# A Mamba mixer and a mixture of experts on one core: routing moved into the mixer's half-steps, the shared expert beside the final sum

## The chip, the cores and the metric

The kernel is one program on one core of a Trainium2 chip. The metric is the device time in microseconds (us) of one execution. Engines are called as in the profile: PE (TensorE), DVE (VectorE), ACT (ScalarE), POOL (GpSimd), SP (SyncE, which issues most DMAs).

## The reference

Two batches of 4096 tokens, 256 features, go through one adaptive-layernorm block of a mixer and a mixture of experts:

```python
mod = (silu(c) @ wmod).reshape(2, 6, 1, 256)       # sa, ca, ga, sb, cb, gb; ga, gb kept at least 0.25 from zero
h = layernorm(x) * (1 + ca) + sa
y = mamba2(h) + h                                  # in-projection, conv of 4 taps, scan over 8 heads x 64 x 128 states,
                                                   # gate by silu(z), rms norm, out-projection
g = y @ glu_w + glu_b;  y = y + g[:256] * sigmoid(g[256:])
x = x + ga * (layernorm(y) * ln_w + ln_b)
h = layernorm(x) * (1 + cb) + sb
scores = sigmoid(h @ gate_w.T);  idx = top4(scores + gate_b);  w = 2.5 * scores[idx] / sum(scores[idx])
y = sum_e w_e * (silu(h @ w1_e) * (h @ w3_e)) @ w2_e      # 16 experts, 4 per token, inner width 128
y = y + (silu(h @ w1_s) * (h @ w3_s)) @ w2_s              # shared expert
out = x + gb * y
```

## The kernel before

Matmuls with weights are made of three products of a high and a low part (`split3`, L102), so a weight or an input is split before its use: ACT makes the high part, DVE or POOL the low part. The engines run by semaphores; each engine's order of work is written out by hand, and an instruction that waits holds all that stands behind it on its engine. `nc.Block` borders, and `clear_semaphores` (L82), are barriers of all engines. The stages in order:

**Setup** (`setup`, L115): DMAs of c, `wmod` and the layernorm weights; ACT takes silu, PE makes the modulation as columns (`mod`) and as rows (the gates), DVE brings them into form.

**Token pass** (`prepare_tokens`, L202): 16 groups of 512 tokens. DVE takes statistics and normalizes, PE turns the tokens (`turn`, L306), ACT modulates, the result goes to `h_dram`; the mixer's weights are split between the groups, and dt and the decays of all tokens are made at the end and stored.

**Mixer** (`mixer`, L464): each batch has 16 steps of 256 tokens (CH = 2 chunks of 128). Both batches run as a pipeline of half-steps: `half(first, second, tail)` (L598 and below) works on three positions at once, the in-projection and conv of one step, the scan of another, the output part of a third; two half-steps advance both batches by one. Each engine has its own `half` with its order: SP L644, PE L796, ACT L927, DVE L1103, POOL L1193. Steps in it that matter below: SP's `load_halves` fills `hN` one half-step ahead, `load_h` fills `hT` (same data) for the residual add; `split_h` splits `hN` into `hTh` and `hTl` (L838 on ACT, L1163 on POOL) for PE's `project_xbc`; `split_y1` makes `y1h` and `y1l` for `glu`; `shift_x` (L1187) prepares the residual; `gated` (L1065), `norm2` and `apply2` (L1087) end the tail; `from_state` (L740) reads the state; `decays` (L882) makes exponentials. The bank names are shared: each batch has four PSUM banks, `Q(b, 0)` to `Q(b, 3)`. The output of the tail, `xr`, goes to `x2_dram`.

**Route** (`route`, L1252): 16 groups of 512 tokens. Loads x2, normalizes and modulates it, takes the scores of 16 experts (`logits`), DVE chooses four (`choose`, `weigh`), PE counts places (`positions`), DVE makes destinations (`assign`), ACT copies each token's row four times with its id and weight beside it (`take_rows`), and POOL scatters them to `xs_dram` with 16 indirect DMAs of 128 rows per group (`scatter`, L1647), sorted by expert. The shared expert is computed for the group too, times the gate, added to x2 and stored to `x2s_dram`, and one expert's weights are loaded (`raw`) and split per group.

**Plan** (`plan`, L1668): from the counts of tokens per expert, a table of 136 pairs of blocks and their weight offsets, read into registers later. **Blocks** (`blocks`, L1761): 136 pairs of 128-row blocks: turn, up, gate, down, scale by the weight, and two indirect scatters of rows to `ys_dram`. **Combine** (`combine`, L2013): 64 tiles of 128 tokens: adds the four expert rows, times the gate, plus `x2s_dram`, to `out`.

Of the kernel before, what the change touches and what calls it, by code (L numbers as in the profile page):

```python
# [16 lines left out]
ALU = mybir.AluOpType  # L17
# [5 lines left out]
NB = 2  # L23
# [25 lines left out]
SERIES = [1.0 / (2 * n + 1) for n in range(8, -1, -1)]  # L49


def build(nc, t, x2_dram, h_dram, par_dram, x2s_dram, xs_dram, ys_dram, out):
# [36 lines left out]
    with ctx:  # L89
# [6 lines left out]
        setup(nc, sem, t, mod, gate_b_row, gate_ln, ident, minus_half, bank)  # L96
        mixer(nc, sem, prime, t, mod, gate_ln, ident, minus_half, bank, h_dram, par_dram, x2_dram)
        clear_semaphores()
        experts(nc, sem, t, mod, gate_b_row, ident, minus_half, bank, x2_dram, x2s_dram, xs_dram, ys_dram, out)
# [15 lines left out]
def setup(nc, sem, t, mod, gate_b_row, gate_ln, ident, minus_half, bank):  # L115

    with ExitStack() as ctx:
        c_col = ctx.enter_context(nc.sbuf_tensor("c_col", [P, KD, NB], F32))
        c_silu = ctx.enter_context(nc.sbuf_tensor("c_silu", [P, KD, NB], F32))
        c_wide = ctx.enter_context(nc.sbuf_tensor("c_wide", [P, KD, NB, P], F32))  # L120
        wmod = ctx.enter_context(nc.sbuf_tensor("wmod", [P, KD, 6 * D], F32))
        pos = ctx.enter_context(nc.sbuf_tensor("pos", [P, 2, D], F32))
        mag = ctx.enter_context(nc.sbuf_tensor("mag", [P, 2, D], F32))
        lnw = ctx.enter_context(nc.sbuf_tensor("lnw", [P, 2, D], F32))
        loaded = sem("mod_loaded")
        silu_done = sem("c_silu_done")
        wide_done = sem("c_wide_done")
        cols_done = sem("mod_cols_done")
        rows_done = sem("mod_rows_done")
        link = sem("mod_link")  # L130
        with nc.Block() as block:
            @block.sync
            def _(sp):
                sp.dma_start(c_col[:, :, :], t["c_col"]).then_inc(loaded, 16)
                sp.dma_start(wmod[:, :, :], t["wmod"]).then_inc(loaded, 16)
                sp.dma_start(ident[:, :], t["ident"]).then_inc(loaded, 16)
                sp.dma_start(lnw[:, :, :], t["ln_wb"]).then_inc(loaded, 16)

            @block.gpsimd
            def _(pool):  # L140
                pool.memset(minus_half[:, :], -0.5)
# [2016 lines left out]
```

## Time and profile before

| | |
|---|---|
| median of 3 timed runs | 2222.96 us (2219.68 to 2231.39) |
| profiled execution, its own time | 2228.17 us |
| its span in the profile | 2226.4 us |
| mean granted TensorE clock | 0.859 |
| busy: PE, DVE, ACT, POOL | 74%, 66%, 47%, 45% |
| moved by DMA | 242.12 MB |

A busy share is that of the span; the clock is 1.0 for 2.4 GHz and 0.5 for 1.2 GHz. The rows that matter stand below, in their section, cut by stage.

### The profile page before, as it was taken

How to read it: one execution, taken by the hardware profiler on the slowest of the kernel's cores; microseconds unless marked ns; L12 is line 12 of the kernel's file. 1: busy time of each engine (PE TensorE's matmuls, PEld its weight loads, DVE VectorE, ACT ScalarE, POOL GpSimd, SP SyncE). 2: the span in 40 equal slices, each digit the busy share in tenths (PEclk: the TensorE clock that was granted, in tenths of full speed). 3: DMA queues.
4: the chain of work that ended last, by engine and by line, in shares of the span. 5: the costliest groups of instructions: out<-in, count | busy, mean ns of one | idle time of the engine just before them, and what ended most of it. 6: DMA issues, size and time to landing. Idle time of an engine off the chain costs nothing. (4 is left out here: it accounts for less than half of the span.)

```text
span 2226.4 us, 37571 instructions
## 1 busy us (share of the span) xinstructions
PE 1658.3 (74%) x10724; PEld 1424.5 (64%) x10725; DVE 1479.1 (66%) x3407; ACT 1053.1 (47%) x2135; POOL 1005.1 (45%) x905
## 2 busy tenths in 40 slices
PE   4757989988999889989887456565319999999300
PEld 4745777777777777777776455454319999999300
DVE  4635788878887788788876566666424444444488
ACT  1315556555655665565564334343206666665200
POOL 1202434443444444334443377777735666666300
PEclk7558999999999999999999666666659999999755
DMA  5421101110111011011010345454334555555599
GB/s 175 153 80 45 35 25 39 39 34 25 39 34 38 26 39 34 24 39 34 29 30 15 115 147 173 145 168 153 131 122 149 177 174 172 176 173 167 211 402 361
DMA packets 148926, 242.12 MB, mean 109 GB/s; under 512 B 24960, under 2 KB 95616, under 8 KB 148608
## 3 DMA queue, kind: packets, MB, share of 16 engines
q1 hardware_dynamic: 122752, 169.77, 24.1%
q0 software_dynamic: 26112, 71.62, 8.8%
q8 instruction: 27, 0.44, 0.1%
q14 instruction: 35, 0.29, 0.0%
HBM read 132.75 MB, written 108.56 MB: 108 GB/s over the span
## 5 line engine op out<-in xcount | busy, mean ns | idle before, releaser
L1997 POOL DMA_INDIRECT ys_dram<-byo,bx x272 | 261.3, 961 | 171.6 <-ACT byo L1930 94.6
L985 DVE SCALAR_TENSOR_TENSOR cv<-xc,convw,cv 128x256 f32<-128x256 f32 x576 | 294.3, 575 | 20.8 <-ACT cv L856 20.8
L1652 POOL DMA_INDIRECT xs_dram<-rows,dest x256 | 264.2, 1032 | 91.9 <-issue 77.1
L1173 POOL TENSOR_TENSOR state<-state,par 128x512 f32<-128x512 f32 x64 | 126.0, 1968 | 283.0 <-PE bank L746 283.0
L1966 DVE TENSOR_TENSOR bff<-bgs,bank 128x256 f32<-128x256 f32 x136 | 57.3, 421 | 212.8 <-ACT bgs L1914 212.8
L1930 ACT ACTIVATE byo<-bank,bx 128x256 f32<-128x256 f32 x272 | 114.3, 472 | 145.3 <-DMA ys_dram<-byo,bx 145.0
L104 PE MATMUL bank<-wh,bhh 128*128 x544 | 160.7, 295 | 8.1 <-ACT bhh L1907 6.0
L106 PE MATMUL bank<-wh,bhl 128*128 x544 | 154.3, 284 | 0.0
L105 PE MATMUL bank<-wl,bhh 128*128 x544 | 153.8, 283 | 0.0
L1184 POOL TENSOR_TENSOR y1l<-y,y1h 128x512 fp32r<-128x512 f32 x32 | 76.2, 2382 | 155.3 <-ACT y1h L912 155.3
L721 PE MATMUL bank<-masked,after 128*128 128x512 f32 x256 | 124.6, 610 | 21.4 <-ACT dec L886 21.4
L104 PE MATMUL bank<-hTh,win_hi 128*128 128x256 f32 x384 | 126.8, 330 | 15.8 <-POOL hTl L1166 15.8
L894 ACT ACTIVATE xdt<-yy 128x512 f32<-128x512 f32 x64 | 40.2, 628 | 192.9 <-POOL yy L1179 192.9
L735 PE MATMUL bank<-xdt,dec 128*128 128x64 f32 x1024 | 121.4, 272 | 0.0
L1179 POOL TENSOR_TENSOR yy<-yy,zs 128x512 f32<-128x512 f32 x64 | 87.6, 1369 | 73.6 <-DVE yy L1039 73.6
L1363 PE MATMUL bank<-ident,xn 128*128 128x128 f32 x128 | 31.5, 427 | 119.3 <-DVE xn L1519 119.3
L735 PEld LDWEIGHTS bank<-xdt,dec 128*128 128x128 f32 x1024 | 119.5, 192 | 0.0
L1907 ACT ACTIVATE bhh<-bank 128x512 fp32r<-128x512 f32 x136 | 83.3, 612 | 74.1 <-PE bank L1838 74.1
L104 PEld LDWEIGHTS bank<-wh,bhh 128*128 128x128 f32 x544 | 103.1, 190 | 18.1 <-issue 17.0
L1957 DVE TENSOR_TENSOR bhl<-bank,bhh 128x512 fp32r<-128x512 f32 x136 | 94.1, 692 | 28.0 <-ACT bhh L1907 24.4
L105 PE MATMUL bank<-hTl,win_hi 128*128 128x256 f32 x384 | 109.5, 285 | 0.0
L106 PE MATMUL bank<-hTh,win_lo 128*128 128x256 f32 x384 | 109.2, 284 | 0.0
(257 smaller groups left out, 5514.0 us busy)
## 6 DMA issues: line engine op xcount, KB each, us to landing
bx<-xs_dram SPq DMA_DIRECT2D x272, 129.0 KB
cy<-ys_dram SPq DMA_DIRECT2D x64, 512.0 KB, 9.2
px<-in_x SPq DMA_DIRECT2D x16, 512.0 KB, 3.6
h_t<-phT SPq DMA_DIRECT2D x16, 512.0 KB, 4.1
hN<-h_t SPq DMA_DIRECT2D x32, 256.0 KB, 2.7
hT<-h_t SPq DMA_DIRECT2D x32, 256.0 KB, 2.6
xr<-in_x SPq DMA_DIRECT2D x32, 256.0 KB, 2.6
x_dram<-xr SPq DMA_DIRECT2D x32, 256.0 KB, 2.0
```

Of the source, the lines that this page charges most:

```text
L104: pe.matmul(out, a_hi, b_hi, start=start, stop=False, skip_group_check=True)
L105: pe.matmul(out, a_hi, b_lo, start=False, stop=False, skip_group_check=True)
L106: return pe.matmul(out, a_lo, b_hi, start=False, stop=stop, skip_group_check=True)
L721: last = pe.matmul(Q(b, 2 + half_heads)[:, :], after[:, :], masked[b][:, c, heads, :].rearrange("p h i -> p (h i)"), start=True, stop=True)
L735: last = pe.matmul(Q(b, c)[:, h * HD:(h + 1) * HD], dec[b][:, c, h, :], xdt[b][:, c, h * HD:(h + 1) * HD], start=False, stop=True, skip_gr ...
L985: dve.scalar_tensor_tensor(cv[b][:, m, :], xc[b][:, m, tap:tap + GROUP], convw[:, m, tap:tap + 1], cv[b][:, m, :], ALU.mult, ALU.add).then ...
L1173: pool.tensor_tensor(s, s, par[b][:, 3, c, :].unsqueeze(2).to_broadcast([P, H, HD]), ALU.mult).then_inc(sdec_done[b], 1)
L1179: pool.tensor_tensor(y, y, zs[b][:, c, :], ALU.mult).then_inc(y4_done[b], 1)
L1652: pool.indirect_dma_start(out=xs_dram[:, :], out_offset=bass.IndirectOffsetOnAxis(ap=dest[n % 2][:, c, k:k + 1], axis=0), in_=rows[n % 2][ ...
L1930: last = act.activation(yo[s % 2][:, n, :], DN[s % 2][:, n * D:(n + 1) * D], ACT.Copy, scale=x[s][:, n, D + 1:D + 2])
L1957: dve.tensor_tensor(hl[par][:, :, :, :].rearrange("p k n t -> p (k n t)"), XT[par][:, :], hh[par][:, :, :, :].rearrange("p k n t -> p (k n ...
L1997: pool.indirect_dma_start(out=ys_dram[:, :], out_offset=bass.IndirectOffsetOnAxis(ap=x[s][:, n, D:D + 1].bitcast(U32), axis=0), in_=yo[s % ...
```

## The change

`setup` and `route` disappear as stages. The modulation is computed in the token pass, around the first group's `turn`: PE does four columns' matmuls in two pairs and the gates' rows after `turn(0)`, DVE `take_mod` and `take_gates` between the groups. A `clear_semaphores` follows the token pass, and the route's constants are loaded with its own.

In the mixer, each half-step takes in up to five parts of routing for older groups, as the new arguments say: `routed` (norm, turn, modulate, logits, tanh for 256 tokens), `chosen` (choose and positions for 512 tokens, every other half-step), `placed` (assign, the half-step after), `copied` (rows of 256 tokens turned and copied four times into the one buffer `rows`), `sent` (eight scatters, in three parts, 3 + 2 + 3). `hN` and its loads go; `split_h` reads `hT`. The two batches share `masked`. The modulated tokens are stored to `h2_dram`. Three more half-steps stand at the end, and the loop body holds four instead of two:

```diff
+    def step(i, p, chosen, sent, last=False):
+        half((1, i), (0, i), (1, i - 1), routed=(0, i - 1, 1 - p), chosen=(i - 2, p) if chosen else None,
+             copied=(1, i - 3, 1 - p) if sent else None, sent=(0, i - 3, 1 - p) if sent else None)
+        half(None if last else (0, i + 1), (1, i), (0, i), routed=(1, i - 1, 1 - p),
+             placed=(i - 2, p) if chosen else None, copied=(0, i - 2, p) if chosen else None,
+             sent=(1, i - 3, 1 - p) if sent else None)
+    half((0, 1), None, None)
     half((1, 1), (0, 1), None)
     half((0, 2), (1, 1), (0, 1))
-    with eng.Fori(2, STEPS) as i:
-        half((1, i), (0, i), (1, i - 1))
-        half((0, i + 1), (1, i), (0, i))
-    half((1, STEPS), (0, STEPS), (1, STEPS - 1), False)
-    half(None, (1, STEPS), (0, STEPS), False)
-    half(None, None, (1, STEPS), False)
+    step(2, 0, False, False)
+    step(3, 1, True, False)
+    with eng.Fori(2, STEPS // 2) as j:
+        step(2 * j, 0, True, True)
+        step(2 * j + 1, 1, True, True)
+    n = STEPS
+    step(n, 0, True, True, True)
+    half(None, None, (1, n), routed=(0, n, 0), chosen=(n - 1, 1), copied=(1, n - 2, 0), sent=(0, n - 2, 0))
+    half(None, None, None, routed=(1, n, 0), placed=(n - 1, 1), copied=(0, n - 1, 1), sent=(1, n - 2, 0))
+    half(None, None, None, chosen=(n, 0), copied=(1, n - 1, 1), sent=(0, n - 1, 1))
+    half(None, None, None, placed=(n, 0), copied=(0, n, 0), sent=(1, n - 1, 1))
+    half(None, None, None, copied=(1, n, 0), sent=(0, n, 0))
+    half(None, None, None, sent=(1, n, 0))
```

On SP:

```diff
         def load_h(b, i):
             sp.wait_ge(y1_done[b], i)
+            sp.wait_ge(hTh_done[b], i)
+            sp.wait_ge(hTl_done[b], i)
...
         def load_again(b, i):
             sp.wait_ge(stored[b], 16 * i)
+            sp.wait_ge(xn_done[b], i)
```

On PE (`turn_x2` turns the normalized tokens, four transposes; `logits` is four matmuls of 16 columns; `turn_rows` four transposes):

```diff
             if second:
                 project_z(*second, 1)
             if tail:
                 project_out(*tail)
             if second:
                 exponents(*second, 0)
+            if routed:
+                turn_x2(*routed)
             if second:
                 x_by_token(*second, 0)
                 x_by_token(*second, 1)
             if tail:
                 state_add(*tail, 1)
+            if routed:
+                logits(*routed)
+            if tail:
                 glu(*tail)
             if second:
                 exponents(*second, 1)
...
             if tail:
                 transpose_y2(*tail)
+            if copied:
+                turn_rows(*copied)
             if second:
                 from_state(*second, 0)
                 state_add(*second, 0)
...
             if first:
...
                 project_xbc(*first, 1)
                 project_xbc(*first, 2)
+            if chosen:
+                positions(*chosen)
             if second:
```

On ACT (`normalize` and `modulate` are two activations each, `score_tanh` one small one):

```diff
         def split_h(b, i):
-            act.wait_ge(hs_in[b], 16 * (i + 1))
+            act.wait_ge(hT_in[b], 16 * (i + 1))
             act.wait_ge(z_ps[b], CH * i)
-            act.activation(hTh[b][:, :, :], hN[b][:, :, :], ACT.Copy).then_inc(hTh_done[b], 1)
+            act.activation(hTh[b][:, :, :], hT[b][:, :, :], ACT.Copy).then_inc(hTh_done[b], 1)
...
+        def copy_rows(b, g, p):
+            act.wait_ge(rows_ps[b], g + 1)
+            act.wait_ge(placed_done, g + 1)
+            if above_zero(g - 1 + b):
+                act.wait_ge(scattered[1 - b], SENT * (g - 1 + b))
+            for k in range(TOPK):
+                act.activation(rows[:, :, k, 0:D], Q(b, 3)[:, :].rearrange("p (c d) -> p c d", c=CH), ACT.Copy)
+            act.activation(rows[:, :, :, D:RW], tail_of[:, CH * b:CH * (b + 1), :, :], ACT.Copy
+                           ).then_inc(rows_done[b], 1)
+            if routed:
+                normalize(*routed)
             if tail:
                 split_y1(*tail)
+            if routed:
+                modulate(*routed)
+            if second:
+                silu_xbc(*second, 2)
+                decays(*second, 0)
+            if routed:
+                score_tanh(*routed)
             if first:
                 split_h(*first)
-            if second:
-                silu_xbc(*second, 2)
-                decays(*second, 0)
             if tail:
                 halve_and_tanh(*tail)
             if second:
...
                 start_conv(*first, 0)
+            if copied:
+                copy_rows(*copied)
             if second:
                 squares(*second, 0)
```

On DVE, with `choose`, `read_positions` and `assign` the chains of route's `choose`, `weigh` and `assign`:

```diff
-        def half(first, second, tail, more=True):
+        def norm3_stats(b, i):
+            dve.wait_ge(xo_done[b], i + 1)
+            for c in range(CH):
+                last = dve.bn_stats(st[b][:, c, :], xr[b][:, c, :])
+            last.then_inc(ln3[b], 1)
+        def norm3_aggr(b, i):
+            dve.wait_ge(ln3[b], 3 * i + 1)
+            stand_alone(dve, held_dve)
+            for c in range(CH):
+                last = dve.bn_aggr(mv[b][:, c, :], st[b][:, c, :])
+            last.then_inc(ln3[b], 1)
+            dve.wait_ge(ln3[b], 3 * i + 2)
+            dve.tensor_scalar(rs[b][:, :], mv[b][:, :, 1], EPS, None, ALU.add).then_inc(ln3[b], 1)
+        def shift_of_norm3(b, g, p):
+            dve.wait_ge(root3[b], g + 1)
+            dve.scalar_tensor_tensor(nmr[b][:, :], mv[b][:, :, 0], -1.0, rs[b][:, :], ALU.mult, ALU.mult
+                                     ).then_inc(nmr_done[b], 1)
...
+            if routed:
+                shift_of_norm3(*routed)
             if second:
                 mask_a(*second, 1)
...
                 for c in range(CH):
                     times_dt(*second, c)
                     times_end(*second, c)
+            if chosen:
+                choose(*chosen)
+            if placed:
+                assign(*placed)
...
             if first:
                 mask_a(*first, 0)
+            if tail:
+                norm3_stats(*tail)
             if second:
                 split_yT(*second, 1)
...
             if second:
                 split_yT(*second, 1)
+            if tail:
+                norm3_aggr(*tail)
             if first:
                 conv(*first, 1)
+            if chosen:
+                read_positions(*chosen)
```

On POOL (`root_norm3` is one small power):

```diff
+        def scatter(b, g, p, part):
+            if part.start == 0:
+                pool.wait_ge(rows_done[b], g + 1)
+                stand_alone(pool, held_pool)
+            for n in range(CH * TOPK)[part]:
+                c, k = divmod(n, TOPK)
+                pool.indirect_dma_start(
+                    out=xs_dram[:, :],
+                    out_offset=bass.IndirectOffsetOnAxis(ap=dest[p][:, CH * b + c, k:k + 1], axis=0),
+                    in_=rows[:, c, k, :], in_offset=None).then_inc(scattered[b], 16)
+        def half(first, second, tail, routed=None, chosen=None, placed=None, copied=None, sent=None):
             if tail:
                 decay_state(*tail, 1)
+            if routed:
+                root_norm3(*routed)
+            if sent:
+                scatter(*sent, slice(0, 3))
             if tail:
+                split_y1(*tail)
                 shift_x(*tail)
-                split_y1(*tail)
+            if sent:
+                scatter(*sent, slice(3, 5))
             if first:
                 split_h(*first)
+            if sent:
+                scatter(*sent, slice(5, 8))
             if second:
                 decay_state(*second, 0)
```

`plan` now also loads and splits all 17 weight sets, in four buffers, ACT the high parts and DVE, behind its own work, the low parts:

```diff
+        for r in range(RAW):
+            sp.dma_start(raw[r][:, :], t["experts"][r]).then_inc(raw_in[r], 16)
         sp.wait_ge(zero_done, 1)
         sp.dma_start(xs_dram[NE * CAP:ROWS, :].rearrange("(n p) d -> p n d", p=P),
                      zero[:, NE:2 * NE, :]).then_inc(spare, 16)
...
+        for r in range(NE + 1):
+            act.wait_ge(raw_in[r % RAW], 16 * (r // RAW + 1))
+            act.activation(wh[:, r, :] if r < NE else sh[:, :], raw[r % RAW][:, :], ACT.Copy).then_inc(hi_done, 1)
...
+        for r in range(NE + 1):
+            hi, lo = (wh[:, r, :], wl[:, r, :]) if r < NE else (sh[:, :], sl[:, :])
+            dve.wait_ge(hi_done, r + 1)
+            dve.tensor_tensor(lo, raw[r % RAW][:, :], hi.bitcast(F32), ALU.subtract).then_inc(lo_done, 1)
```

`blocks` casts the two ids of a pair on DVE (`take_ids`), and POOL's scatter waits for it. `combine` loads the modulated tokens, computes the shared expert for 16 groups of 512 tokens (ACT and POOL split, PE, silu, DVE's product), adds on DVE two and two of four rows (`pair`, 128x1024) and sums those on PE by the identity into the shared expert's bank; DVE multiplies by the gate and adds x2, which comes from `x2_dram`. Rows of y come by 1 MB:

```diff
+        def add_up(g):
+            pe.wait_ge(fh_done, g + 1)
+            pe.wait_ge(fl_done, g + 1)
+            for n in (2 * g, 2 * g + 1):
+                if n >= 4:
+                    pe.wait_ge(gated, n - 3)
+                for c in range(2):
+                    tok = slice((n % 2 * 2 + c) * P, (n % 2 * 2 + c + 1) * P)
+                    split3(pe, TOTAL[n % 4][:, c * D:(c + 1) * D], fh[g % 2][:, tok], fl[g % 2][:, tok],
+                           w2(sh), w2(sl), c == 0, False)
+                pe.wait_ge(pair_done, n + 1)
+                for m in range(2):
+                    last = pe.matmul(TOTAL[n % 4][:, :].rearrange("p (c d) -> p c d", c=2), ident[:, :],
+                                     pair[n % 2][:, :, m, :], start=False, stop=(m == 1),
+                                     skip_group_check=True)
+                last.then_inc(total_ps, 1)
```

## Rows read from the trace of the kernel before

**Rows 1.** Windows by stage: stretch, length, busy (x count) of PE, PEld, DVE, ACT, POOL; clock; DMA share; GB/s.
```profile
0.00:29.30 29.30, 12.88 (x48) 11.47 (x49) 9.39 (x24) 2.12 (x3) 0.29 (x5) 0.92 0.18 65
29.30:168.60 139.30, 87.06 (x390) 82.48 (x390) 74.21 (x242) 32.82 (x42) 20.84 (x20) 0.51 0.43 149
168.60:1234.80 1066.20, 940.86 (x5952) 753.27 (x5952) 840.53 (x1568) 610.72 (x1152) 426.44 (x320) 0.98 0.11 33
1234.80:1623.50 388.70, 208.79 (x1056) 187.28 (x1056) 235.41 (x883) 145.64 (x258) 280.84 (x272) 0.67 0.45 149
1623.50:1659.00 35.50, 3.33 (x14) 1.85 (x14) 12.30 (x26) 0.00 (x0) 15.40 (x16) 0.50 0.38 122
1659.00:2093.50 434.50, 405.37 (x3264) 388.11 (x3264) 195.89 (x408) 261.81 (x680) 261.31 (x272) 0.98 0.54 165
2093.50:2226.40 132.90, 0.00 (x0) 0.00 (x0) 111.35 (x256) 0.00 (x0) 0.00 (x0) 0.50 0.99 379
```

**Rows 2.** Route's row scatters: their group, their DMA issues, two in the timeline.
```profile
L1652 POOL DMA_INDIRECT xs_dram<-rows,dest x256 | 264.2, 1032 | 91.9 <-issue 77.1
...
xs_dram<-rows,dest POOLq DMA_INDIRECT x256, 3.0
...
1315.22 0.96 POOL L1652 DMA_INDIRECT xs_dram<-rows,dest  x1 [0.30 <-issue]
1316.49 1.64 POOL L1652 DMA_INDIRECT xs_dram<-rows,dest  x1 [0.30 <-issue]
```

**Rows 3.** One half-step of the mixer: its window, then its timeline (start, us, engine, operation).
```profile
707.40:739.25 31.85, 28.99 (x188) 23.28 (x187) 25.75 (x49) 19.11 (x36) 13.68 (x10) 1.00 0.11 34
...
730.21 0.68 DVE L1062 TENSOR_TENSOR y<-bank,hT 128x512 f32<-128x512 f32 x1
731.46 0.62 ACT L841 ACTIVATE hTh<-hN 128x512 fp32r<-128x512 f32 x1
731.63 2.77 POOL L1184 TENSOR_TENSOR y1l<-y,y1h 128x512 fp32r<-128x512 f32 x1 [4.75 <-ACT y1h L912]
738.77 0.68 PE L104 MATMUL bank<-hTh,win_hi 128*128 128x256 f32 x1
739.25 0.69 DVE L1067 SCALAR_TENSOR_TENSOR sg<-sg,xend 128x512 f32<-128x512 f32 x1 [3.00 <-ACT sg L923]
741.30 0.60 PE L792 MATMUL bank<-ident,y 128*128 128x128 f32 x4
742.49 0.67 PE L746 MATMUL bank<-state,cv 128*128 128x512 f32 x1 [0.59 <-DVE gm L1017]
```

**Rows 4.** DVE's norm statistics, choosing and assigning (windows of DVE alone); ACT's copy of rows.
```profile
710.40:711.76 1.36, 1.17 (x7) 1.00 0.00 0
1295.76:1299.61 3.85, 3.22 (x24) 0.50 0.72 192
1302.46:1304.94 2.48, 2.20 (x10) 0.93 0.28 102
...
1293.10 4.03 ACT L1461 ACTIVATE rows<-bank 128x512 f32<-128x512 f32 x8 [0.32 <-PE bank L1392]
```

**Rows 5.** Timeline at the end of the mixer.
```profile
1218.66 1.26 POOL L1184 TENSOR_TENSOR y1l<-y,y1h 128x512 fp32r<-128x512 f32 x1 [7.13 <-ACT y1h L912]
...
1229.65 0.88 DVE L1099 SCALAR_TENSOR_TENSOR xr<-sg,rs,xr 128x256 f32<-128x256 f32 x2
```

**Rows 6.** Timeline of PE in setup and at the start of the token pass.
```profile
16.45 6.04 PE L165 MATMUL bank<-wmod,c_wide 128*128 128x256 f32 x16
...
38.23 1.94 PE L312 MATMUL bank<-ident,px 128*128 128x128 f32 x8 [15.74 <-DVE px L394]
```

**Rows 7.** Plan's last cast; the loads of the expert weights; DVE's low parts in route.
```profile
1640.55 0.42 DVE L1748 CAST weights_at<-bank 1x272 int32<-1x272 f32 x1
...
raw<-in_experts SPq DMA_DIRECT2D x17, 384.0 KB, 5.4
...
L1618 DVE TENSOR_TENSOR wl<-raw,wh 128x768 fp32r<-128x768 f32 x16 | 15.1, 946 | 0.0
```

More of the change, by code:

```diff
@@ L507, in mixer @@
         btok = both("btok", [P, CH, NS])
-        masked = both("masked", [P, CH, H, P])
+        masked = [sb(f"masked{c}", [P, H, P]) for c in range(CH)]
         dec = both("dec", [P, CH, H, P])
@@ L794, in transpose_y2, with turn_x2 @@
                     last.then_inc(y2T_ps[b], 1)
-                def half(first, second, tail, more=True):
+                def turn_x2(b, g, p):
+                    pe.wait_ge(xn_done[b], g + 1)
+                    pe.wait_ge(yTl_done[1 - b], up_to(CH * (g + b) + 1, CH * (STEPS + 1)))
+                    pe.wait_ge(tanh2_done[b], g)
+                    xn = sg[b][:, :, :].rearrange("p k t -> p (k t)")
+                    for k in range(KD):
+                        for c in range(CH):
+                            last = pe.transpose(Q(1 - b, 0)[:, k * GROUP + c * P:k * GROUP + (c + 1) * P],
+                                                xn[:, c * D + k * P:c * D + (k + 1) * P], ident[:, :])
+                    last.then_inc(xT2_ps[b], 1)
@@ L797, in half @@
+                def half(first, second, tail, routed=None, chosen=None, placed=None, copied=None, sent=None):
                     if second:
@@ L1104, in half @@
+                def half(first, second, tail, routed=None, chosen=None, placed=None, copied=None, sent=None):
+                    if routed:
+                        shift_of_norm3(*routed)
                     if second:
@@ L1248, in experts @@
-        blocks(nc, sem, ident, bank, wh, wl, rows_at, weights_at, xs_dram, ys_dram)
-        combine(nc, sem, gate_b_row, x2s_dram, ys_dram, out)
-def route(nc, sem, t, mod, gate_b_row, ident, minus_half, bank, wh, wl, run, x2_dram, x2s_dram, xs_dram):
-    GROUPS = NB * MSTEPS
-    XBUF = 3
-    RAW = 2
-    with ExitStack() as ctx:
-        def sb(name, shape, dt=F32):
-            return ctx.enter_context(nc.sbuf_tensor(name, shape, dt))
-        def two(name, shape, dt=F32):
-            return [sb(f"{name}{b}", shape, dt) for b in range(2)]
-        raw = [sb(f"raw{r}", [P, EW]) for r in range(RAW)]
@@ L1308, in route @@
-        (stats, aggr, eps, root, xn_done, xT_ps, hT_done, hh_done, hl_done, logit_ps, tanh_done, mask_done, pos_ps,
-         run_done, dest_done, rows_ps, rows_done, gate_ps, up_ps, gs_done, ff_done, fh_done, fl_done,
-         down_ps, gated, added, hi_done, lo_done, link, held, consts, _, _, pos_read) = (sem("r_" + n) for n in names)
-        x2_in = [sem(f"r_x2_in{n}") for n in range(XBUF)]
-        raw_in = [sem(f"r_raw_in{n}") for n in range(RAW)]
-        scattered = [sem(f"r_scattered{n}") for n in range(2)]
@@ L1667, in plan @@
+        combine(nc, sem, gate_b_row, ident, bank, sh, sl, h2_dram, x2_dram, ys_dram, out)
+def plan(nc, sem, t, ident, bank, run, wh, wl, sh, sl, rows_at, weights_at, xs_dram):
+    RAW = 4
     with ExitStack() as ctx:
@@ L1984, in step @@
                         split_x(u + 2, par)
-                split_x(0, 0)
-                split_x(1, 1)
+                        take_ids(u + 2, *later(s, i, 2))
+                for u in range(2):
+                    split_x(u, u)
+                    take_ids(u, u, 0)
                 walk(dve, step)
```

1043 lines of the change are left out of this document (491 added, 552 removed).

## The prediction

> **What bounds the kernel now.** I read the per-core line first: one core, span 2226.4 us. The profiled execution took 2228.17, so 1.8 lie around the span, and the median of the timed runs, 2222.96, is 5.2 less; the sum below is made against the span. The page's busy shares (PE 74%, DVE 66%) average over seven stages with different limits, so I cut the span into windows at the stages' borders [rows 1]. Read there: the mixer is half of the time, with PE busy 941 of 1066 and DVE 841; the route stage (388.7) has no engine above 73% and a clock of 0.67, so it waits on dependencies; the blocks are PE's (405 of 434.5); combine is the DMA's (share 0.99 at 379 GB/s) with PE, ACT and POOL idle. The change takes a whole stage away and pushes its parts into stages that are full on one engine only. What each part costs is read inside the stage that receives it.
>
> **Route goes: −388.7** [rows 1]. Its work has to reappear, and the next four terms price it.
>
> **Half-steps of the mixer: +2.6 each, 30 of them, +78.** A half-step lasts 31.85, with PE busy 28.99, DVE 25.75, ACT 19.1, POOL 13.7 [rows 3]. Added per half-step: on PE eight transposes (two groups of four at 0.60, [rows 3]), four tiny logits matmuls (~0.3) and half a `positions` (~0.2): 1.7, so 30.7. On DVE the statistics of 256 tokens (1.36), the shift (0.2), and half of choosing and of assigning for 512 tokens, (3.85 + 2.5 + 0.4)/2 = 3.4 with `read_positions` [rows 4]: 4.95, so 30.7. On ACT four copies of 128x512 at 0.5 (8 took 4.03, [rows 4]) and the copy of the ids (0.2), plus normalize, modulate and tanh (~2.2): 4.5, so 23.6. On POOL a small root and eight row scatters, issued 1.27 apart [rows 2], 10.9, so 24.6. Every engine still fits into 31.85, so it is order that sets the growth. I followed the stretch that binds. DVE does `norm3_aggr` and `shift_of_norm3` (all but the statistics proper of the 1.36 in [rows 4], and one small operation, 0.85 to 1.0) before the y1 add of 730.21, so `glu` and the waits behind it come 0.9 later. `hN` is gone, so `split_h` cannot run early at 731.46: it stands behind normalize, modulate, `decays(0)` and `score_tanh`, some 738.15, and POOL's `hTl` (1.3) behind `shift_x` and two scatters, to 739.2 to 740.5. So `project_xbc` of pair 0, at 738.77 before, starts at ~740.6. `turn_rows` comes behind it (0.6, partly in the present idle ahead of `from_state`), and `from_state` moves from 742.49 to ~744.4: +1.9. `positions` on PE and DVE's answer add ~0.3, and scatters that run slow beside DVE ~0.4. Sum 2.6. Bounds: if all but the PE work fits in slack, 1.2 (half-step 33.1); if choose and assign fall entirely on DVE's path, 5 (37). I take 2.6, since the shift of pair 0's matmuls is a wait of the written order, while `choose` and `assign` stand where DVE waits for PE. SP's queue: `load_again` now waits for normalize, and `load_par` and `load_h` of the next group stand behind it; `load_h` lands ~2.6 after issue, still ahead of ACT's turn to split.
>
> **Drain: +71.** Each of the six trailing half-steps only routes, copies or sends, and `rows` has one buffer: copy waits until the other batch's eight scatters have landed. In the first, y1l ends at 1219.9 [rows 5], five more scatters follow, the last begins at 1226.3 and lands 3.0 later [rows 2], the copy takes 2.2, so sends of the second start at ~1232.7. From then on one cycle is 7 × 1.267 + 3.0 + 2.2 + 0.3 (waits) = 14.4. Four cycles and a last 8.87 + 3.0 end at 1302.2, against 1230.9 for the old end (DVE's last operation ends 1230.5, [rows 5]): +71. Bounds: 55 (landing hidden) to 85 (scatters at 1.64).
>
> **Setup folded in: −12.** PE's `mod_rows` run 16.45 to 22.5 and the first `turn` only at 38.23 to 40.2 [rows 6]. In the new order the weight of the modulation lands at ~9, eight small matmuls 3.5, turn(0) 2, eight more 3.5, rows 6.0: turn(1) at ~25.3, 15 earlier. `take_gates`, ~4.4 twice on DVE (most of its 9.39 in the setup window, [rows 1]), now stands within the groups and gives back ~3. Bounds −15 to −4 (if the stage is held by its loads, DMA share 0.43, [rows 1]).
>
> **One more clearing and more semaphores to prime: +3**; bounds 1 and 5. **Plan: +11.** 17 sets of 384 KB go through 4 buffers here; the first four are loaded at once, DVE reaches the low parts after its last cast (1640.55, 17 in, [rows 7]). 13 sets in cycles of four, each landing (5.4 among other traffic, [rows 7]; I take 3.8, between that and a scatter's 3.0, since the queue is free here) + ACT + DVE 0.95: 29 to 35 after 17.4, so 46.5 to 50 instead of 35.5; I take 46.5. Bounds +8.5 and +14.7, by a landing a little shorter and by 5.4. **Blocks: +1**: one small cast on DVE, busy 196 of 434, and one wait on POOL, which waits for ACT's rows anyway; PE covers both. Without cover 5.
>
> **Combine: +24.** 50.3 MB took 132.9 at 379 GB/s [rows 1]. The shared expert's input adds 8.4 MB: 22, plus ~2 for filling. Its engines: a group of 512 tokens has the product of two block pairs. A pair costs PE 405.4/136 = 2.98, so a group 6.0 at the full clock [rows 1], and with 4 identity matmuls for the pairs against the turns of the blocks ~6.3, below the DMA's 156.9/16 = 9.8. But at 0.50, the clock of [rows 1] for stages in which PE is little busy, it is 11.9, 190 in all. Bounds +22 and +57.
>
> **Sum**: 2226.4 − 388.7 + 78 + 71 − 12 + 3 + 11 + 1 + 24 = 2013.7; + 1.8 around the span − 5.2 to the median: 2010.
>
> **A rule against this change.** A row first: POOL's y1l takes 2.77 beside DVE's conv [rows 3] and 1.26 alone [rows 5], a scatter 1.64 beside DVE and 0.96 else, 1.03 in the mean [rows 2], while DVE's wl, run in the same stage as these scatters, keeps 0.946 [rows 7]. So in this trace POOL pays, not DVE. The Trainium skill, page "SBUF — State Buffer", section "SBUF: two separate sides", says that VectorE and GpSimd share a port pair under an exclusive lock, held for a whole instruction, when DVE runs in a two-port mode or reads two SBUF inputs. By that rule POOL's added work would stop DVE as well; the trace agrees as to POOL and shows no case for DVE.
>
> **Rivals.**
> *R1, POOL or DVE becomes the bound of the half-step.* Eight scatters hold DVE for their 0.96 each, 7.7: DVE's 30.7 becomes up to 38.4; with three quarters of it, 36.5. For it: DVE has only 3.8 of slack at 34.45, and its added operations are linked chains of small ones. Against: wl's 0.946. Time: 2010 + 30 × (36.5 to 38.7 − 34.45) = 2072 to 2138.
> *R2, combine bound by PE at half clock.* PE would be idle a third of each group, as it is in the stages at 0.50 to 0.67. Price 57 for 24: 2043.
> *R3, the additions vanish in idle time.* PE's path waits 31.85 − 28.99 = 2.9 per half-step; if most of the growth fits, the half-step is 32.9: 2010 − 30 × 1.55 = 1963.
> *R4, slower than before.* One mechanism: with more waits per half-step PE's clock falls to 1.2 GHz in the mixer, as in the token pass (0.51 with PE busy 87 of 139, [rows 1]). At half clock PE's 30.7 becomes 61. The change loses from 2010 + 213: a half-step of 34.45 + 7.1 = 41.6, which is 23% of half-steps at the low clock. Against: the mixer has 0.98, and PE's busy share goes only from 91% to 89%; the low-clock stages have 54 to 63%.
> That route doesn't really go is no rival: its work is out of the stage, and only where it lands counts.
>
> **How the numbers follow.** Forecast 0.56 (its own range 1985 to 2040, from the bounds of drain, plan and ±0.7 per half-step), R1 0.20, R2 0.12, R3 0.08, R4 0.04. Predicted 2010. The range goes from 1960, just under R3, to 2090, which takes in R2 and the near part of R1; outside are the far part of R1, R4 and the tails, below 0.2. Faster by over 0.5%: all but R4, less 0.01 for the edge, 0.95; within 0.5% (about what a measurement of this kernel can tell from no change) 0.01; slower 0.04.
>
> **What would show it.** Half-step: the spacing of DVE's gated operation in the loop, 34.45; 36.5 or more is R1, with DVE operations stretched beside scatters; below 33, R3; a granted clock under 0.9 there, R4. Drain: scatter cycles 14.4 apart after the mixer's last y1l, with ACT's copy waiting on the landing. The token pass: turn(1) at ~25 instead of 40. Plan: 46 from its first transfer, and DVE's low parts last. Combine: 157, DMA share near 0.99 and GB/s near 375; with PE busy over 90% and a clock of 0.50, R2. Wrong would be the prediction if the half-step's growth is set by a wait that I walked past, since 1 us there is 30.

## The result and the profile after

The changed kernel takes 2264.02 us (median of 4, 2257.98 to 2265.33) against 2221.32 (median of 4) before: ratio 1.0179, 95% interval 1.0141 to 1.0218. It is 1.8% slower, clear of the noise, where 2010 was forecast. The profiled execution has a span of 2263.5 against 2226.4.

Windows of the changed kernel by stage, in the columns of [rows 1]: token pass; mixer with the routing in it and the drain; plan; blocks; combine.

```profile
0.00:143.10 143.10, 94.31 (x438) 89.42 (x439) 82.80 (x267) 34.73 (x45) 19.91 (x21) 0.62 0.47 160
143.10:1402.90 1259.80, 1051.10 (x6624) 853.15 (x6624) 1032.52 (x2288) 743.00 (x1472) 698.80 (x614) 0.93 0.17 56
1402.90:1446.80 43.90, 3.33 (x14) 1.84 (x14) 28.00 (x43) 14.24 (x17) 19.85 (x16) 0.54 0.80 251
1446.80:1883.00 436.20, 404.72 (x3264) 385.89 (x3264) 206.66 (x544) 262.01 (x681) 261.64 (x272) 0.97 0.54 165
1883.00:2263.50 380.50, 161.59 (x512) 107.44 (x512) 88.74 (x112) 34.86 (x48) 58.62 (x32) 0.69 0.44 155
```

The last line is the news. Combine took 132.9 at a DMA share of 0.99 [rows 1]; now it takes 380.5 at 0.44, with PE busy for 162, DVE for 89. No engine is full and the DMAs aren't either, so they wait for each other. With borders taken at the same events in both traces (the mixer's first memset, the first and the last `gated`, the ends of the stages), the forecast's terms and the measured ones are:

| | forecast | measured |
|---|---|---|
| start of the mixer (pass, clearing, priming) | −12 + 3 | −20.1 |
| half-steps, first to last `gated` | +78 | +113.5 |
| drain | +71 | +74.2 |
| route | −388.7 | −388.8 |
| plan | +11 | +9.1 |
| blocks | +1 | +1.3 |
| combine | +24 | +247.3 |
| sum (with +0.6 ahead of the first `gated`) | −212.7 | +37.1 |

**Combine, one group.** Timeline of the changed kernel, one turn of the circle, rows of SP, ACT, POOL, PE and DVE put in order of time:

```profile
2074.29 0.68 DVE L2093 TENSOR_TENSOR cx<-cx,ctotal 128x512 f32<-128x512 f32 x1
...
2075.00 0.38 SPq L1977 DMA_DIRECT2D out<-cx  x1
...
2075.97 1.58 SPq L1970 DMA_DIRECT2D cy<-ys_dram  x2
...
2077.59 0.69 SPq L1963 DMA_DIRECT2D chT<-h_dram  x1
...
2087.25 1.06 ACT L2042 ACTIVATE chh<-chT 128x1024 fp32r<-128x1024 f32 x1 [18.52 <-DMA chT<-h_dram]
...
2088.38 2.34 POOL L2112 TENSOR_TENSOR chl<-chT,chh 128x1024 fp32r<-128x1024 f32 x1 [22.05 <-ACT chh L2042]
...
2090.82 0.77 PE L115 MATMUL bank<-chh,shared_hi 128*128 128x512 f32 x1 [14.98 <-issue]
...
2095.93 0.69 DVE L2077 TENSOR_TENSOR cff<-cgs,bank 128x512 f32<-128x512 f32 x1 [19.82 <-issue]
...
2099.47 0.68 DVE L2093 TENSOR_TENSOR cx<-cx,ctotal 128x512 f32<-128x512 f32 x1
```

Read it from the top: DVE's last sum of a group lets SP issue the store; behind it SP asks for x2, for two times 1 MB of y, and last for the tokens `chT`. These requests take SP 2.6. The tokens land 9.7 later, behind the 2.5 MB of loads ahead of them. Then come 1.06 + 2.34 for the split, 5.2 for the twelve matmuls and 4.2 for DVE's products and sums, and only then the next store: 25.2 in all. In the code: `store(g)` waits for `add_x2(2g+1)`, which stands on DVE behind `times(g+2)`, which needs `up(g+2)`, whose tokens SP requested just ahead of that store. Two buffers look like a load in advance; by the orders of SP and DVE there is none.

**Half-step.** Window of one, then the two rows at a jump back of the loop, then the page's line on instruction loads (packets, MB, share):

```profile
1033.30:1068.63 35.33, 32.22 (x212) 26.24 (x212) 32.57 (x67) 23.02 (x46) 20.63 (x19) 1.00 0.17 58
...
502.27 0.77 PE L115 MATMUL bank<-win_hi,hTh 128*128 128x512 f32 x1 [3.64 <-issue]
...
505.44 0.16 DVE L1302 SCALAR_TENSOR_TENSOR nmr<-mv,rs 128x2 f32<-128x2 f32 x1 [2.63 <-issue]
...
q8 instruction: 79, 1.29, 0.2%
```

Against [rows 3] the half-step is 3.5 longer, not 2.6, with DVE busy for 32.6 where 30.7 was forecast. And after each of the five jumps back (six turns of the loop) one half-step takes 38.9 to 41.5: PE and DVE stand still for 3.6 and 2.6 "for issue", right behind their branch.

Beside DVE's conv, POOL's two tensor operations now stand back to back. Timeline rows of DVE (six undisturbed conv operations, then the six beside POOL's two) and of POOL, then the conv's group on the page:

```profile
1052.58 2.47 DVE L1167 SCALAR_TENSOR_TENSOR cv<-xc,convw,cv 128x256 f32<-128x256 f32 x6
1056.91 5.32 DVE L1167 SCALAR_TENSOR_TENSOR cv<-xc,convw,cv 128x256 f32<-128x256 f32 x6
...
1058.64 1.28 POOL L1464 TENSOR_TENSOR y1l<-y,y1h 128x512 fp32r<-128x512 f32 x1
1059.86 1.29 POOL L1469 TENSOR_TENSOR xr<-xr,gate_ln 128x512 f32<-128x512 f32 x1
...
L1167 DVE SCALAR_TENSOR_TENSOR cv<-xc,convw,cv 128x256 f32<-128x256 f32 x576 | 338.9, 655 | 22.5 <-ACT cv L995 22.5
```

A conv operation takes 0.475 undisturbed, and six of them 2.47, since they overlap a little. The second six take 2.85 more, about the length of POOL's two operations: one of them starts 0.54 before POOL's first and ends 0.3 behind POOL's second, and lasts 3.34 to 3.35. That is so in 21 half-steps; in the five behind a jump back, where the operations meet otherwise, two conv operations last 1.5 each instead. The same line of the kernel before, on its page:

```profile
L985 DVE SCALAR_TENSOR_TENSOR cv<-xc,convw,cv 128x256 f32<-128x256 f32 x576 | 294.3, 575 | 20.8 <-ACT cv L856 20.8
```

So DVE paid before, too: 47 of its 576 conv operations took 1.5 and 31 took 0.8, all 78 beside a tensor operation of POOL.

**The rest.** In the token pass PE turns the second group at 24.43 (25.3 forecast, 42.78 before). In the drain ACT's copies wait for the landing, as forecast, and stand 14.4 to 16.4 apart; rows of ACT and POOL:

```profile
1338.55 2.07 ACT L1097 ACTIVATE rows<-bank 128x512 f32<-128x512 f32 x4 [3.95 <-DMA xs_dram<-rows,dest]
1354.94 2.07 ACT L1097 ACTIVATE rows<-bank 128x512 f32<-128x512 f32 x4 [14.23 <-DMA xs_dram<-rows,dest]
...
1352.34 0.96 POOL L1483 DMA_INDIRECT xs_dram<-rows,dest  x1 [0.30 <-issue]
1357.93 0.96 POOL L1483 DMA_INDIRECT xs_dram<-rows,dest  x1 [4.62 <-ACT rows L1098]
```

### The profile page after: what moved, and what is told of

The parts are those of the page before. It is cut to its first block and busy times, and to the rows that moved or that the text cites. A ratio compares the mean times of both kernels' runs of the same rounds, so it can differ in the third digit from the quotient of the medians.

```text
span 2263.5 us, 37959 instructions
## 1 busy us (share of the span) xinstructions
PE 1715.0 (76%) x10852; PEld 1437.8 (64%) x10853; DVE 1438.7 (64%) x3254; ACT 1088.8 (48%) x2263; POOL 1058.8 (47%) x954
## 3 DMA queue, kind: packets, MB, share of 16 engines
q8 instruction: 79, 1.29, 0.2%
## 5 line engine op out<-in xcount | busy, mean ns | idle before, releaser
L1167 DVE SCALAR_TENSOR_TENSOR cv<-xc,convw,cv 128x256 f32<-128x256 f32 x576 | 338.9, 655 | 22.5 <-ACT cv L995 22.5
L1903 POOL DMA_INDIRECT ys_dram<-byo,bids x272 | 261.6, 962 | 177.1 <-ACT byo L1829 94.7
L1483 POOL DMA_INDIRECT xs_dram<-rows,dest x256 | 279.6, 1092 | 87.7 <-issue 69.2
L115 PE MATMUL bank<-chh,shared_hi 128*128 128x512 f32 x64 | 40.2, 629 | 223.9 <-issue 201.2
L2112 POOL TENSOR_TENSOR chl<-chT,chh 128x1024 fp32r<-128x1024 f32 x16 | 37.5, 2343 | 309.4 <-ACT chh L2042 309.4
L804 PE MATMUL bank<-masked,after 128*128 128x512 f32 x256 | 135.9, 657 | 54.5 <-ACT dec L1025 54.5
L115 PEld LDWEIGHTS bank<-chh,shared_hi 128*128 128x128 f32 x64 | 19.7, 308 | 240.1 <-issue 235.7
L1453 POOL TENSOR_TENSOR state<-state,par 128x512 f32<-128x512 f32 x64 | 109.2, 1707 | 81.8 <-PE bank L829 81.7
L2042 ACT ACTIVATE chh<-chT 128x1024 fp32r<-128x1024 f32 x16 | 16.9, 1056 | 258.1 <-DMA chT<-h_dram 258.1
L1737 PE MATMUL bank<-ident,bx 128*128 128x128 f32 x544 | 84.7, 279 | 37.4 <-DMA bx<-xs_dram 36.4
```

Of the source, the lines that this page charges most:

```text
L115: pe.matmul(out, a_hi, b_hi, start=start, stop=False, skip_group_check=True)
L804: last = pe.matmul(Q(b, 2 + half_heads)[:, :], after[:, :], masked[c][:, heads, :].rearrange("p h i -> p (h i)"), start=True, stop=True)
L1167: dve.scalar_tensor_tensor(cv[b][:, m, :], xc[b][:, m, tap:tap + GROUP], convw[:, m, tap:tap + 1], cv[b][:, m, :], ALU.mult, ALU.add).then ...
L1453: pool.tensor_tensor(s, s, par[b][:, 3, c, :].unsqueeze(2).to_broadcast([P, H, HD]), ALU.mult).then_inc(sdec_done[b], 1)
L1483: pool.indirect_dma_start(out=xs_dram[:, :], out_offset=bass.IndirectOffsetOnAxis(ap=dest[p][:, CH * b + c, k:k + 1], axis=0), in_=rows[:, ...
L1737: last = pe.transpose(XT[s % 2][:, (k * 2 + n) * P:(k * 2 + n + 1) * P], x[s][:, n, k * P:(k + 1) * P], ident[:, :])
```

## The experiments

The first four ran on the same chip as the two kernels. The later ones ran on another, where the kernel before takes 2356 to 2381 and the blocks take 527 to 538 instead of 434 to 437 in every kernel. The other stages of the changed kernel agree on the two chips: first to last `gated` 1111.1 and 1112.1 (x6), combine with two buffers 380 and 377 (x5). The kernel before loses time there in its route stage as well: in x8, the one kept trace of such a kernel on that chip, the time from the last `gated` to the last row scatter is 453.9, where x3 has 391.5. So totals are compared only within a chip, and stages of the changed kernel across; a ratio to before on the second chip flatters every changed kernel.

### Combine: one more group ahead (x1_h_ahead)

```diff
-        hT = several(2, "chT", [P, KD, MGROUP])
+        hT = several(3, "chT", [P, KD, MGROUP])
...
-                    if g + 2 < GROUPS:
-                        load_h(g + 2)
+                    if g + 3 < GROUPS:
+                        load_h(g + 3)
```

> The changed kernel with a third buffer for the modulated tokens in combine, so that they are requested one group earlier. Theory (closed loop): in combine each store waits for work that waits for the tokens requested just ahead of it, so one landing (9.4), the split (1.06 + 2.34), the matmuls (5) and DVE's sums (4.2) follow each other in every group, 25.3 us. Then combine falls from 378 to 157 to 175, DMA share over 0.9, total 2045 to 2065. Rival A (TensorE at 1.2 GHz sets the group): about 190 for combine, TensorE busy over 90%, total 2075 or more. Rival B (larger loads of y are slow by themselves, or instruction supply starves the engines): combine stays over 300.

2104.8, ratio to before 0.9477 (0.9446 to 0.9509): 159 less by one buffer. Window of its combine:

```profile
1887.10:2106.80 219.70, 144.96 (x512) 94.41 (x512) 109.92 (x112) 35.02 (x48) 67.64 (x32) 0.82 0.74 268
```

The buffer takes away what the circle cost only in part: 220 is more than the 157 to 175 expected. It is 13.7 a group, about half of 25.2, as if the same chain, spread over two groups, still set the pace.

### Combine: the request first in its queue (x2_h_first)

```diff
+                    if g + 2 < GROUPS:
+                        load_h(g + 2)
                     for n in (2 * g + YBUF, 2 * g + YBUF + 1):
                         if n < HALVES:
                             load_y(n)
-                    if g + 2 < GROUPS:
-                        load_h(g + 2)
```

> The changed kernel with the same two buffers, but the request for the modulated tokens stands ahead of the two 1 MB loads of y in the queue. Closed loop: the landing falls from 9.4 to about 4 to 5 and the request is 1.6 earlier, so a group takes 18 to 20 instead of 25.3 and combine 290 to 320, total 2180 to 2205. Rival (bandwidth or TensorE sets the group): no change, since bytes and matmuls are the same.

2191.4 in its one run. The window of combine and the group of the tokens' DMA issues (count, KB, median to landing), which was 9.5 in the changed kernel:

```profile
1883.60:2189.50 305.90, 162.56 (x512) 108.16 (x512) 88.91 (x112) 34.86 (x48) 59.66 (x32) 0.75 0.54 192
...
chT<-h_dram SPq DMA_DIRECT2D x16, 512.0 KB, 6.0
```

Bytes, matmuls and buffers are the same. The landing is 3.5 shorter (4.5 to 5.5 were expected) and the request 1.6 earlier: 5.1 per group, 82 for 16, and 74.6 were gained. A stage that was bound by bandwidth or by PE would not have moved.

### Combine: three groups ahead (x6_h4)

The edit of x1 with four buffers and `load_h(g + 4)`.

> The changed kernel with four buffers for the modulated tokens in combine instead of two, requested three groups ahead of their use where the original is one ahead. With three buffers combine fell from 380 to 220, 13.7 per group, about half of 25.3: the same chain of 25.3 spread over two groups. Theory: spread over three it is 8.4, under the transfers' 9.8, so that the DMAs set the group: combine 157 to 170, DMA share over 0.95, total 2045 to 2060. Rival (TensorE sets the rest: 6.9 to 11 per group by its clock): combine 180 to 215.

Windows of its combine, and of 50 us in its middle:

```profile
1975.50:2153.20 177.70, 129.63 (x512) 86.30 (x512) 120.95 (x112) 35.12 (x48) 66.59 (x32) 0.95 0.93 331
2050.00:2100.00 50.00, 39.37 (x160) 26.26 (x160) 37.73 (x35) 10.98 (x15) 21.23 (x11) 1.00 1.01 360
```

So combine takes 380, 220 and 178 with two, three and four buffers. In the 50 us shown of the last the DMAs are full and PE is at 79%, at the full clock. The 178 is 8 over the range: the DMAs move 331 GB/s over the stage (308 from 2000 to 2050, 344 to 360 behind it) where 375 was counted on, and the first and last group are slow. The total, 2153.7, is 0.9136 of before on the second chip (0.9115 to 0.9157).

### POOL: shift_x behind the middle scatters (x4_shift_later)

```diff
                         split_y1(*tail)
-                        shift_x(*tail)
                     if sent:
                         scatter(*sent, slice(3, 5))
+                    if tail:
+                        shift_x(*tail)
```

> The changed kernel with shift_x on POOL behind the two middle scatters instead of right behind split_y1. Theory (the two tensor operations of POOL, back to back, hold one conv operation of DVE for 3.35 instead of 0.47): separated, the conv operation beside y1l takes 1.5, and shift_x holds another operation for at most 1.0 or none, so the half-step falls by 0.5 to 1.9 (from 35.3), 30 of them: total 15 to 55 less than 2264. Rival (DVE is not what sets the half-step): conv gets shorter but the half-step stays 35.3, total unchanged.

2226.3, 38 less than the changed kernel and 1.0016 of before (0.9996 to 1.0036). Its page:

```profile
L1167 DVE SCALAR_TENSOR_TENSOR cv<-xc,convw,cv 128x256 f32<-128x256 f32 x576 | 307.9, 601 | 22.8 <-ACT cv L995 22.7
```

The conv operation of 3.35 now takes 2.1: it still starts 0.54 before `y1l` and ends 0.3 behind it. Most half-steps take 34.0 to 34.4 instead of 35.3 to 35.7, and from the first to the last `gated` 1070.4 instead of 1111.1. All this comes from the order of two operations on an engine that is busy 60% of the time.

### The loop: is it the length of the body? (x3_before_body4, x5_unrolled, x8_before_body6)

The kernel before with four half-steps in the body:

```diff
-            with eng.Fori(2, STEPS) as i:
-                half((1, i), (0, i), (1, i - 1))
-                half((0, i + 1), (1, i), (0, i))
+            with eng.Fori(1, STEPS // 2) as j:
+                for i in (2 * j, 2 * j + 1):
+                    half((1, i), (0, i), (1, i - 1))
+                    half((0, i + 1), (1, i), (0, i))
```

> The kernel before, with a loop body of four half-steps instead of two (7 turns instead of 14) and nothing else changed. Theory (the longer body has to be fetched again at each jump back): one half-step in four is 4 to 5 longer, as in the changed kernel (40.2 against 35.3), 7 x 4.5 = +30, total about 2250. Rival (the long half-steps of the changed kernel come from its added work, such as a wait that falls on the first half-step of the body): all half-steps stay at 31.85 to 32.5, total unchanged within 0.5%.

2225.9, ratio 1.0013 (0.9993 to 1.0032), no half-step longer than before: my theory as I had put it, that four half-steps are too many, fell. But from one jump back to the next that body has 1587 records of PE in the trace (weight loads and sequencer included) and 338 of DVE; in the changed kernel it is 1779 and 475. So the changed kernel with its loop written out:

```diff
-            with eng.Fori(2, STEPS // 2) as j:
+            for j in range(2, STEPS // 2):
```

> The changed kernel with the mixer's loop of six turns (four half-steps each) written out, no jump back. Theory (TensorE's and VectorE's instructions after the jump have to be fetched, 3.9 and 3.2 us in which they issue nothing): the long half-steps of 38.9 to 41.5 become 35.3 to 36.7, 6 x 4.5 = 27 less, total about 2237. Rival A (the long half-step comes from a wait in the order that the body holds, whoever jumps): spacings stay as they are, total 2264. Rival B (straight code is fetched too slowly as well): all half-steps grow and the total is over 2264.

2335.0, ratio 0.9905 (0.9882 to 0.9929), on the second chip. The long half-steps are gone (35.2 to 37.3 where the loop was). From the first to the last `gated` it takes 1093.7 instead of 1111.1, which is 17 of the expected 27: there are five jumps, not six, and every other half-step is 36.5 where it was 35.6. With these 17 put back the changed kernel would take about 2352 on this chip, an estimate, which is no slower than before there. And the kernel before with a body of six half-steps (steps 3 to 14 in four turns, 2 and 15 written out):

> The kernel before with six half-steps in the loop body (the first and last pair of half-steps written out, four turns), nothing else changed. With four half-steps its body showed no stall; TensorE's part of it is about 1600 records, that of the changed kernel's about 1780 and with a stall at each jump. Theory (the stall comes with the length of the body alone): six half-steps are about 2400 records, over the changed kernel's, so one half-step in six after each of three jumps is 3 to 5 longer (35 to 37 against 31.9). Rival (the stall needs something else of the changed kernel): all stay at 31.9 to 32.5.

Timeline rows of DVE at its first jump back, and the instruction loads of its page:

```profile
484.56 0.69 DVE L1073 SCALAR_TENSOR_TENSOR sg<-sg,xend 128x512 f32<-128x512 f32 x1 [3.00 <-ACT sg L929]
508.89 1.23 DVE L999 TENSOR_TENSOR masked<-upto,par 128x1024 f32<-128x1024 f32 x1 [2.60 <-issue]
521.83 0.69 DVE L1073 SCALAR_TENSOR_TENSOR sg<-sg,xend 128x512 f32<-128x512 f32 x1 [1.57 <-ACT sg L929]
...
q8 instruction: 74, 1.21, 0.2%
```

It takes 2407.1 in its one run, against 2380.6 before on that chip. The half-steps behind the three jumps take 37.3, 36.5 and 36.9, most of the others 31.8 to 32.7. There are 74 loads of instructions where the body of four had 30 (and the kernel before 27), a part of them because more half-steps stand written out. A turn has 2378 records of PE and 499 of DVE. No work was added, only length. So it is the length of the body; what fits lies between 1587 and 1779 records for PE, or between 338 and 475 for DVE, since the runs don't tell which of the two decides.

### All three (x7_joined, x10_joined_again)

> The changed kernel with all three edits: four buffers for the modulated tokens in combine, shift_x behind the middle scatters, the mixer's loop written out. If the three causes are separate, the gains add up: 380 to 165 in combine (215), 38 for shift_x, 27 for the jumps: 2264 - 280 = 1984, range 1970 to 2000. If two of them share a cover (the jumps' stalls give way to DVE's chain once that is shorter), 10 to 20 of it is missing.

2088.3, ratio 0.8858 (0.8843 to 0.8873); once more, in another comparison on that chip:

> The kernel with all three edits once more, beside the one above and on the same chip: half-step 34.0, combine 165 to 178. If the blocks take 436 on this chip as in the first kernels, about 1995 in all, otherwise about 2088.

2096.5, ratio 0.8802 (0.8778 to 0.8825). The gains add up: combine 177.4, first to last `gated` 1048.0 (63 less than the changed kernel: 41 of x4 and 17 of x5 and 5 more). With its blocks at 436 the span of 2088.8 would be 1997, an estimate of the time on the first chip: 0.90 of before, and not 0.88 to 0.89.

### What sets the half-step now? (x9_split_early, x11_stats_twice, x12_turn_twice)

On the joined kernel. First the step that the prediction had named, ACT's order:

```diff
+                    if first:
+                        split_h(*first)
                     if second:
                         silu_xbc(*second, 2)
                         decays(*second, 0)
                     if routed:
                         score_tanh(*routed)
-                    if first:
-                        split_h(*first)
```

> The kernel with all three edits, and ACT's split_h ahead of silu_xbc(2), decays(0) and score_tanh again, right behind modulate. The prediction named this order as the step that sets the half-step's growth (pair 0 of project_xbc 1.9 later). Theory P (the order of split_h sets it): the half-step falls from 34.0 by 1 to 1.9, total 30 to 55 less than the kernel with three edits. Theory D (DVE, busy 31 of 34, sets it since it has the added operations, and PE waits for DVE's conv and sums): half-step 33.8 to 34.2, total within 0.3%, or up to 0.5 per half-step longer as silu_xbc is later.

2136.4, ratio 0.8956 (0.8923 to 0.8990), is 40 more than x10 beside it: neither theory. ACT's split, as its source line tells it:

```profile
L980 ACT ACTIVATE hTh<-hT x32: 627/632/636, 152.5 to 1218.7; 128x512 fp32r<-128x512 f32 x32
its engine sat idle before it (us, times) until:
  DMA hT<-h_t: 93.3, 28
```

There is no buffer filled ahead any more, so an early split waits 3.3 for its load, and all behind it on ACT too. This run therefore doesn't tell what an early split would give with its load in time. Then a cost doubled on DVE (the tail's statistics taken a second time, into a tile that nobody reads) and one on PE (each transpose of `turn_x2` made twice):

> The kernel with all three edits, and DVE takes the statistics of the tail's 256 tokens twice (once into a tile that nobody reads), +0.65 to 0.7 per half-step on DVE. Theory D (DVE's order sets the half-step): half-step 34.0 + 0.6 to 0.7 = 34.6 to 34.7. Theory E (PE or ACT sets it and DVE has room there): less than 34.2.

> The kernel with all three edits, and PE turns the 256 normalized tokens twice (turn_x2 with each transpose made two times), +0.5 to 0.6 per half-step on PE. Theory D (DVE's order sets the half-step, PE has room in front of its waits): half-step at most 34.2. Theory E (PE's order sets it): 34.5 to 34.6. If both this and the run above are longer, the limit changes from engine to engine along the half-step, and neither alone is the bound.

Windows from one `gated` to the one two half-steps later, of x7, x11 and x12 in this order:

```profile
986.27:1054.33 68.06, 63.17 (x416) 51.35 (x414) 63.33 (x143) 46.37 (x92) 44.37 (x39) 1.00 0.19 64
```

```profile
995.81:1064.68 68.87, 63.10 (x415) 51.36 (x414) 64.16 (x148) 46.51 (x92) 44.39 (x39) 1.00 0.19 64
```

```profile
990.05:1058.11 68.06, 64.00 (x424) 52.25 (x422) 63.34 (x143) 46.35 (x92) 44.36 (x39) 1.00 0.19 64
```

They are 68.06, 68.87 and 68.06 long. In x11 DVE is busy 0.83 longer for two half-steps, and they take 0.81 more. In x12 PE is busy 0.83 longer, and they take no more, though PE is busy for 31.6 of 34.0, as long as DVE (31.7). Over twenty half-steps of the loop the mean is 34.08 in x10, 34.55 in x11 and 34.11 in x12. So DVE's order sets the pace at the place where this cost was added, and PE's does not at its own; other places of the two orders were not tried. The totals, one run each, are 2115.0 and 2102.9 against 2096.5.

## Why the prediction was wrong

**The step that failed: "Combine: +24"** ("The shared expert's input adds 8.4 MB: 22, plus ~2 for filling"). I sized the stage by its bytes and by PE's work. With four buffers it is 178 where these gave 157: the DMAs are busy for 0.93 of it, but move 331 GB/s where 379 was counted on. PE, at the full clock, is not in the way, so rival R2 is out. What I didn't do for this stage is what I did for the half-step, to walk the orders of the queues. The code of the change shows all of it: `load_h` last in SP's turn, the store behind it, `times(n // 2 + 1)` on DVE ahead of the sums of the group before. The circle costs 380.5 − 177.7 = 203; without it the +37 would have been −166. The remaining 45 of combine (177.7 against 132.9) are 21 over the forecast 24, by the lower GB/s and the slow ends. x2 shows the circle by the order of the requests alone, x1 and x6 by the number of buffers.

**"Half-steps: +2.6 each"** was off by two terms that are not in the sum. One is POOL: `split_y1` and `shift_x` back to back hold DVE's conv (x4: 41 of the 113.5). The other is the jump back of a longer body (x5, x8: about 17 to 25). Without both the half-step is 34.0 to 34.1, +2.2 for the forecast 2.6. That the size came near is in part luck, for most of it was put on the later `split_h` ("+1.9"), and the trace doesn't bear that out: in 25 half-steps of the changed kernel (300 to 1200) PE waits 3.2 in all for `hTl` ahead of `project_xbc`, and in the joined kernel at most 0.3. x11 shows that most of a cost on DVE counts where it was tried (0.47 of 0.6), and x12 that PE's doesn't. Which waits make up the whole of the 2.2 stays open.

**R1** (POOL holds DVE) had the right pair and the wrong operations. Conv operations beside a scatter alone take 0.474 in the mean, those beside nothing 0.475 (188 and 175 of them): scatters alone don't hold DVE. POOL's tensor operations do. "POOL pays, not DVE" was wrong, since the evidence stood in the kernel before: its conv group has a mean of 575 where the undisturbed operation has 475. The Trainium skill, page "SBUF — State Buffer", section "SBUF: two separate sides", says that the shared port pair is held for a whole instruction; for a DVE operation with two SBUF inputs it limits this to GpSimd operations that read SBUF. The trace agrees as far as tensor operations go: the conv operation of 3.34 spans two of POOL's, 1.28 and 1.29. It shows no such hold for the scatters, by which I had priced the rival.

**R4**, the opposite side, named the clock, which stayed at 0.97 from the first to the last `gated` (1.00 in the half-step shown). The kernel did become slower, but by another way. **R3** did not come: no addition vanished.

**The token pass** gave 20, not 9. `turn(1)` is near where it was put (24.43 for 25.3), but the 15 were taken against 40.2, which is the end of `turn(0)`; `turn(1)` itself stood at 42.78, so it comes 18.4 earlier. By the fifth group the lead is 20.6 (37.76 against 58.34), and so it is in the last (107.36 against 127.91): `take_gates` gives nothing back, and the clearing and priming take 0.4 of it, not 3. Why 2 more were won behind `turn(1)` was not tested. **Drain, plan, blocks, route** came within 3.2 of their terms.

Two things stay open: why the written-out loop of x5 has half-steps of 36.5 where the loop had 35.6, and which of PE's and DVE's stalls at the jump decides. The Trainium skill, page "Runtime: NRT & Kernel Launch", section "Instruction fetch mechanics", says that an engine's store of instructions is small (2048 for TensorE, 512 for most others), refilled in blocks of 256, and that a taken branch whose target lies outside the current two blocks waits for a load. The runs agree in kind, but not in the figures: the stall is there at 1779 records of PE and 475 of DVE, under 2048 and 512, and PE has none at 1587, over two blocks. The blocks' borders or records missing from the trace may have a part in this; no run shows it.

## What to carry to other kernels

A stage that gets a new producer must be walked for circles: for each load, find the instruction that its request stands behind, and follow whether that one waits for this load's own consumer. Bytes and busy time bound a stage only when no such chain is longer; buffers count by how many groups lie between request and use in the orders of all engines. Look in the trace for operations with two lengths (0.475 and 1.5): what runs beside the longer ones says which neighbour holds them, and two such neighbours back to back cost the sum. A loop body can grow until its jump back costs 3 to 6 us. And when runs come from two chips, compare stage by stage: a ratio can move because the kernel before has a stage that one of the chips runs slower.

## What the runs showed of the hardware

One DVE operation of 0.475 took 3.35 beside two POOL tensor operations back to back, and 1.5 or (x4) 2.1 beside one, but 0.474 beside indirect DMAs issued by POOL. A loop body of 1587 PE and 338 DVE records jumped back without a stall; one of 1779 and 475, and one of 2378 and 499, cost 3 to 6 us at each jump. And the blocks stage, block loads and row scatters at 165 GB/s, took 434 to 437 on one chip and 527 to 538 on another, for a cause that no run shows. The route stage of the kernel before took about 60 longer there as well, while mixer and combine agreed within 2%.
